# Attended values of a cross-attention kernel: transposed token-major by DMA, and an output projection on scaled 16-bit parts

## The reference

```
q    = x @ W_q                      k_t, v_t  = text @ W_k, text @ W_v
p_t  = softmax(q k_t^T / sqrt(32))  text_out  = p_t v_t
qsem = l2norm(p_t @ text)           sem       = qsem . l2norm(image)
p_ip = softmax(q k_ip^T / sqrt(32) + 0.5 * sem) * mask      ip_out = p_ip v_ip
out  = (text_out + ip_out) @ W_out + b_out + x
```

## Time and profile before

| | us |
|---|---|
| median of 3 runs | 1199.03 |
| profiled execution, whole | 1194.57 |
| its span | 1192.8 |
| busy DVE | 959.0 (80%) |
| busy ACT | 726.2 (61%) |
| busy POOL | 533.0 (45%) |
| busy DMA engines, queue q1 | 54.9% |

### The profile page before, as it was taken

How to read it: one execution, slowest core, us unless ns; L and a number is a source line. 1 busy time by engine, 2 the same in 40 slices (tenths; PEclk the granted TensorE clock), 3 DMA queues, 4 the chain that set the end, 5 groups by cost and what they waited for, 6 DMA issues and landing times.

```text
span 1192.8 us, 27846 instructions
## 1 busy us (share of the span) xinstructions
PE 1102.1 (92%) x8149; PEld 977.1 (82%) x8149; DVE 959.0 (80%) x3834; ACT 726.2 (61%) x2299; POOL 533.0 (45%) x1774
## 2 busy tenths in 40 slices
PE   6993777999999999999999999999999999999977
PEld 5862666888888888888988889888888898888867
DVE  3243488889888988989888988988898988898972
ACT  1142576767666666767676767666666767676630
POOL 0001254455554454555455455455445545545540
PEclk9797889999999999999999999999999999999989
DMA  9586645545465657464645546464756474555421
GB/s 298 193 150 151 140 90 117 121 105 150 106 160 125 152 106 157 105 147 107 142 123 126 156 103 161 109 144 97 159 128 164 103 149 120 131 116 106 112 76 56
DMA packets 386607, 156.91 MB, mean 132 GB/s; under 512 B 354057, under 2 KB 363557, under 8 KB 386457
## 3 DMA queue, kind: packets, MB, share of 16 engines
q1 hardware_dynamic: 386457, 155.14, 54.9%
HBM read 43.15 MB, written 28.05 MB: 60 GB/s over the span
## 4 chain that ended last, share of the span: by engine, by line
PE 30%; DVE 24%; issue 9%; DMA 9%; ACT 8%; POOL 8%; SPq 0%; DVEq 0%; ACTq 0%
PE ps_O L1098 12%; PE ps_Q L1065 9%; DMA pts<-ph 9%; ACT pr L812 4%; PE ps_S L1025 4%; DVE smax L911 3%; PE ps_U L1041 3%; ACT ph L775 3%; DVE pr L961 3%; POOL ph L840 3%; DVE xT_lo L889 2%; DVE aT L929 2%; DVE attn L984 2%; DVE n L973 2%; DVE bias L921 2%
## 5 line engine op out<-in xcount | busy, mean ns | idle before, releaser
L812 ACT ACTIVATE pr<-ps_S,bias 128x73 f32<-128x73 f32 x1280 | 305.4, 322 | 260.8 <-DVE bias L921 260.0
L840 POOL TENSOR_TENSOR ph<-pr,ph 128x220 f16<-128x220 f32 (+1 forms) x640 | 281.2, 460 | 312.3 <-ACT ph L775 307.7
L1098 PE MATMUL ps_O<-wo_hi,aT 128*128 128x320 f32 x1240 | 332.1, 325 | 36.2 <-DVE x_in L902 21.5
L775 ACT ACTIVATE ph<-pr 128x292 f16<-128x292 f32 x640 | 252.0, 444 | 65.8 <-DMA pts<-ph 56.8
L1098 PEld LDWEIGHTS ps_O<-wo_hi,aT 128*128 128x128 f32 x1240 | 219.5, 190 | 51.5 <-DVE x_in L902 29.5
L1025 PE MATMUL ps_S<-kbd,qT 128*128 128x308 f32 x960 | 203.0, 321 | 0.9 <-ACT pr L812 0.7
L1098 PE MATMUL ps_O<-wo_lo,aT 128*128 128x320 f32 x620 | 192.7, 311 | 0.0
L1041 PE MATMUL ps_U<-xm,pts 128*128 128x110 f16 (+1 forms) x2560 | 187.4, 216 | 3.7 <-DVE attn L984 2.2
L911 DVE TENSOR_REDUCE smax<-ps_S 128x4 f32<-128x292 f32 x320 | 145.6, 455 | 50.4 <-PE ps_S L1025 50.0
L1065 PE MATMUL ps_Q<-xT_hi,wq_hi 128*128 128x512 f32 x400 | 162.2, 405 | 12.3 <-DVE qT L889 12.2
L1065 PE MATMUL ps_Q<-xT_lo,wq_hi 128*128 128x512 f32 x400 | 165.9, 415 | 0.0
(11 more groups left out here) (169 smaller groups left out, 1629.6 us busy)
## 6 DMA issues: line engine op xcount, KB each, us to landing
x_in<-in_x_dram SPq DMA_DIRECT2D x16, 1280.0 KB, 6.4
out_dram<-x_in SPq DMA_DIRECT2D x64, 320.0 KB, 2.7
pts<-ph SPq DMA_TRANSPOSE x320, 2.8
w_k<-in_L_xattn_W_k_dram SPq DMA_DIRECT2D x5, 512.0 KB, 9.0
w_ip<-in_L_xattn_W_k_ip_dram SPq DMA_DIRECT2D x1, 2560.0 KB, 11.9
w_v<-in_L_xattn_W_v_dram SPq DMA_DIRECT2D x1, 2560.0 KB, 20.8
w_ip<-in_L_xattn_W_v_ip_dram SPq DMA_DIRECT2D x1, 2560.0 KB, 10.3
xm<-x_d SPq DMA_DIRECT2D x20, 110.0 KB
```

The lines of the kernel that those rows point to most:

```text
L775: last = nc.scalar.activation(hi[:, :, col:col + T], pr[u % P_RING][:], ACT.Copy)
L812: last = nc.scalar.activation(pr[t % P_RING][:, h, :], sc[:, h, 0:T], ACT.Exp, bias=bias[t % 2][:, h:h + 1], scale=SCALE)
L840: nc.gpsimd.tensor_tensor(lo, pr[u % P_RING][:, :, t0:t1], one[:, :, 0, t0:t1], ALU.subtract).then_inc(pl_ready, 1)
L1098: last = nc.tensor.matmul(bank[m][:, 0:HALF], stationary[:, q * P:(q + 1) * P], moving, start=(k, a, b_) == O_MMS[0], stop=(k, a, b_) == O ...
```

## The change

The attended values are no longer transposed on TensorE. `attn` (128 tokens x 4 x 128, float32) is split into 16-bit parts as it lies, token by token: ScalarE writes the high part `at16[:, 0]` at s = 0 of the slot two later, GpSimd the low part `at16[:, 1]` (one instruction of 128x512) at s = 1 behind its two pieces of `ph`, and SP issues one DMA transpose of 128x1024 at s = 2 into a ring of 10. The output projection multiplies 16-bit `aT` with 16-bit `wo`, both scaled by powers of two; the image values `vw` and the bias are scaled alike, in float32. Each output add multiplies by `inv_out`. In ScalarE's order the new instruction stands behind L775 and ahead of what `finished` lists and of L812; SP's new transpose stands behind that of `ph` in the same step. In the prologue the high part of `W_out` is made later, and its maximum is taken to find the scale.

```diff
-        if s == 1 and w.has(slot - 2):
-            todo.append(("attn", slot - 2, 0, 0, "M"))
...
+                    if s == 2 and w.has(slot - 2):
+                        m = slot - 2
+                        ring = w.count(SLOTS, m) % AT_RING
+                        sp.wait_ge(at_hi, w.count(SLOTS, m + 1))
+                        sp.wait_ge(at_lo, w.count(SLOTS, m + 1))
+                        if w.has(m - AT_RING):
+                            sp.wait_ge(o_ready, w.count(NI * OUTS, OUTS * ((m - AT_RING) // CC + 1)))
+                        sp.dma_start_transpose(aT[ring][:], at16[m % 2][:].rearrange("p k s c -> p (k s c)")
+                                               ).then_inc(aT_loaded[ring], 16)
...
+                    if s == 0 and w.has(slot - 2):
+                        m = slot - 2
+                        act.wait_ge(attn_ready, w.count(UNITS, SUB * (m + 1)))
+                        if w.has(m - 2):
+                            old = w.count(SLOTS, m - 2)
+                            act.wait_ge(aT_loaded[old % AT_RING], 16 * (old // AT_RING + 1))
+                        nc.scalar.activation(at16[m % 2][:, 0], attn[m % 2][:].rearrange("p s h d -> p s (h d)"),
+                                             ACT.Copy).then_inc(at_hi, 1)
...
-                            nc.scalar.activation(aT[w.count(SLOTS, i) % AT_RING][0][:], ps_M[:], ACT.Copy, scale=inv_sv).then_inc(aT_hi, 1)
...
+                    if s == 1 and w.has(slot - 2):
+                        m = slot - 2
+                        pool.wait_ge(at_hi, w.count(SLOTS, m + 1))
+                        nc.gpsimd.tensor_tensor(at16[m % 2][:, 1], attn[m % 2][:].rearrange("p s h d -> p s (h d)"),
+                                                at16[m % 2][:, 0], ALU.subtract).then_inc(at_lo, 1)
...
-                            nc.vector.tensor_tensor(half, bank[m][:, 0:HALF], half, ALU.add).then_inc(o_added, 1)
+                            nc.vector.scalar_tensor_tensor(out=half, in0=bank[m][:, 0:HALF], scalar=inv_out, in1=half,
+                                                           op0=ALU.mult, op1=ALU.add).then_inc(o_added, 1)
...
-                            nc.vector.scalar_tensor_tensor(out=aT[w.count(SLOTS, i) % AT_RING][1][:], in0=ps_M[:], scalar=inv_sv,
-                                                           in1=aT[w.count(SLOTS, i) % AT_RING][0][:].bitcast(F32),
-                                                           op0=ALU.mult, op1=ALU.subtract).then_inc(aT_lo, 1)
...
-                            for q in range(SUB):
-                                last = nc.tensor.transpose(ps_M[:, q * P:(q + 1) * P],
-                                                           attn[i % 2][:, q].rearrange("p h d -> p (h d)"), ident[:])
...
-                            if part == 0:
-                                pe.wait_ge(aT_lo, w.count(SLOTS, CC * (i + 1)))
+                            for k in ((0, 1, 2), (3, 4))[part] if c == 0 else ():
+                                n = w.count(SLOTS, CC * i + k)
+                                pe.wait_ge(aT_loaded[n % AT_RING], 16 * (n // AT_RING + 1))
```

More of the change, by code:

```diff
@@ L226, in _ @@
                 nc.gpsimd.memset(vip_bd[:], 0.0).then_inc(bd_zero, 1)
-                for k in range(2):
+                for k, (total, own) in enumerate(((2, 0), (14, 13), (3, 1))):
                     pool.wait_ge(local_max, k + 1)
-                    nc.gpsimd.partition_all_reduce(amax[:, 2 + k:3 + k], amax[:, k:k + 1], P, RMAX).then_inc(all_max, 1)
+                    nc.gpsimd.partition_all_reduce(amax[:, total:total + 1], amax[:, own:own + 1], P, RMAX).then_inc(all_max, 1)
             @block.scalar
@@ L554, in main_loop @@
     OUTS = 2 * SUB
-    AT_RING, P_RING, SIP_RING, PH_RING, PT_RING = 9, 5, 3, 2, 3
+    AT_RING, P_RING, SIP_RING, PH_RING, PT_RING = 10, 5, 3, 2, 3
     X_RING = NI
@@ L591, in main_loop @@
     attn = [sb(f"attn{i}", [P, SUB, HG, DH], F32) for i in range(2)]
-    aT = [[sb(f"aT{r}_{k}", [P, TILE], F32R) for k in range(2)] for r in range(AT_RING)]
+    at16 = [sb(f"at16_{i}", [P, 2, SUB, P], F16) for i in range(2)]
+    aT = [sb(f"aT{r}", [P, 2 * SUB, P], F16) for r in range(AT_RING)]
     pip = sb("pip", [P, SUB, IPR + 1], F32)
@@ L611, in main_loop @@
         sem(n) for n in "u_ready nd_done prod_done rd_done n2_done attn_ready".split())
-    aT_ready, aT_hi, aT_lo = sem("aT_ready"), sem("aT_hi_done"), sem("aT_lo_done")
+    at_hi, at_lo = sem("at_hi_done"), sem("at_lo_done")
+    aT_loaded = [sem(f"aT_loaded{r}") for r in range(AT_RING)]
     n2h_done, y0_ready, newton_step, y_ready = (sem(n) for n in "n2h_done y0_ready newton_step y_ready".split())
@@ L672, in emptied @@
         return {"x": (xT_lo, w.count(SLOTS, CC * i + c + 1)), "q": (q_lo, w.count(SLOTS, i + 1)),
-                "attn": (aT_lo, w.count(SLOTS, i + 1)), "ip": (pT_lo, w.count(NI, i + 1)),
+                "ip": (pT_lo, w.count(NI, i + 1)),
                 "out": (o_added, w.count(NI * OUTS, OUTS * i + c + 1))}[kind]
@@ L982, in turn @@
                         if w.has(un - 2) and us == 0:
-                            v.wait_ge(aT_ready, w.count(SLOTS, un - 1))
+                            v.wait_ge(at_hi, w.count(SLOTS, un - 1))
+                            v.wait_ge(at_lo, w.count(SLOTS, un - 1))
                         nc.vector.tensor_tensor(attn[un % 2][:, us], uo[:, :, COL_V:XW],
@@ L1067, in turn @@
                             last.then_inc(q_ready, 1)
-                        elif kind == "attn":
-                            pe.wait_ge(attn_ready, w.count(UNITS, SUB * (i + 1)))
-                            for q in range(SUB):
-                                last = nc.tensor.transpose(ps_M[:, q * P:(q + 1) * P],
-                                                           attn[i % 2][:, q].rearrange("p h d -> p (h d)"), ident[:])
-                            last.then_inc(aT_ready, 1)
                         elif kind == "ip":
```

68 lines of the change are left out of this document (38 added, 30 removed).

## The result

The changed kernel takes 1239.72 us in the median of 4 runs (1236.14 to 1243.81), the kernel before 1199.99 beside it: ratio 1.032, 95% interval 1.028 to 1.036. The change makes the kernel some 40 us slower. The forecast was 1214, 15 us slower: the right side, and 1.3 us inside the range's upper end of 1241, but well short in size. The profiled execution spans 1242.0 us.

What follows compares the result with a forecast made beforehand. A once-per-slot loop of VectorE, ScalarE and GpSimd, 12.36 us without TensorE, was taken as the bound. Terms summed to +0.22 us a slot, +15 us in all: 1209.6 profiled, median 1214 us, 8-in-10 range 1178 to 1241.

Steps and rivals of the forecast that it cites:

- hold by the low part: At s = 1, GpSimd's 128x512 instruction keeps VectorE's f (L968) waiting for its end: +0.70 us a slot, bounds 0.57 to 0.85.
- bias: VectorE's bias of s = 3, held by GpSimd's later first piece of ph: +0.08 us a slot, +0.37 if for both pieces.
- L929 removed: VectorE's L929 leaves what was read as a gapless stretch of the loop: -0.66 us per slot.
- the add: VectorE's output add gets a scalar operand: +0.06 us each, about one in the stretch, so +0.05 us a slot.
- ScalarE's new copy: ScalarE's 128x512 instruction at s = 0 behind L775, 0.6 us long: +0.05 us a slot, bounds 0 to 0.25.
- DMA transposes, with the waits for them: SP's extra transpose per slot, behind the pts transpose, lands two steps ahead of the piece needing it: nothing.
- Rival (a): No hold on VectorE's f (L968), so the loop loses 0.61 us a slot: 1150 us; chance 0.15.
- the gapless stretch: VectorE works without a gap from w_sem to the bias of s = 3, which ends 6.14 us after y.
- The loop without TensorE: Once per slot, from y through VectorE, ScalarE and GpSimd's Newton rounds: 12.36 us, with no instruction of TensorE in it.
- Rival (c): DMA: 80 more transposes make ScalarE wait 0.4 us more a slot for pts transposes: 1246 us; chance 0.15.
- TensorE's relief: Four transposes, 0.43 us per slot, leave TensorE outside the loop; earlier scores give about 2 us less over the run.
- the added waits: ScalarE's for attn_ready at s = 0, GpSimd's for at_hi and SP's for at_lo: nothing.

Runs made afterwards that it cites:

- the stub kernel: The changed kernel with GpSimd's new low-part instruction writing 16 of 512 columns only: 0.999 to the kernel before, 1197.65 us.
- a third kernel: The changed kernel with 16-column low part, all added per-slot pieces left out from the tenth slot on: 0.986; with TensorE's four transposes put back, unread: 0.984.

## Why the prediction was right in its sign and wrong in its size

Steps from kernel to kernel, in us a slot (1% of 1199 us over 80 slots is 0.15), against the terms of the sum:

| term | forecast | measured | from |
|---|---|---|---|
| hold by the low part | +0.70, bias +0.08 | +0.50 (alone in before: +0.70) | 1.032 less 0.999 |
| L929 removed | -0.66 | -0.14 for 0.46 of it on average | 0.991 |
| the same, and three of TensorE's four transposes | -0.66 and 2 us in all | -0.12 | 0.992 |
| the rest of L929 and of the transposes, 16-bit outputs, ScalarE's old copy gone, the prologue | +0.05, for the add | -0.10 | 0.986 less 0.992, intervals overlap |
| ScalarE's new copy (and the stub) | +0.05 | 0.0 | 0.985 less 0.986 |
| DMA transposes, with the waits for them | 0 | +0.21 | 0.999 less 0.985 |

All rows but the second (it is part of the third) add up, as they must, to the whole: +0.48 a slot before rounding, 39 us. The 0.46 is 37 us over 80 slots.

- **The hold** was right in mechanism and place, and with the bias too high in size: 0.78 against 0.50. That the kernel before with the added instruction gave 0.70, just as forecast, is in part luck: that instruction takes 1280 ns and not 1119, f was held 0.95, and ScalarE waited for it too. GpSimd's instruction takes 1158 ns; 1119 came from the slope of the earlier trace rows. f's median is 794 ns against "0.7 us or more", and in the slot shown f ends 0.08 us behind it. The Trainium skill, GPSIMD Engine Reference, Specifications, tells of contention on the shared SBUF interfaces; by that rule, the trace agrees, and adds that the VectorE instruction is not slowed but kept to the other's end. Rival (a) fell with it.
- **L929 is the mis-sized term,** and the largest error. All removals together, with the 16-bit outputs, measured -0.21 (0.986) where I had -0.61: 0.40 us a slot too favourable, and of L929 by itself three tenths came out. With the transposes' 0.21 this outweighs what I had too high elsewhere (hold and bias 0.28, ScalarE's copy 0.05 or so), and leaves the 0.26 by which +0.22 fell short of +0.48. The step that failed was "it lies in the gapless stretch: -0.66 us per slot". The stretch was gapless in the slot that I showed. The slots come in rounds of five with different TensorE work and transfers, and the waits ahead of smax, qT and pipT in the others were not among what I read: of the waits has only ScalarE's for pts and w_sem's for y. Over the run, VectorE could give up 0.52 us a slot and have seven tenths of it waited away at the next wait.
- **The loop without TensorE** was the premise behind that step, and it too was read in one slot. The page of before, part 4, gives the shares of the chain that ended last, over the whole run:

```profile
PE 30%; DVE 24%; issue 9%; DMA 9%; ACT 8%; POOL 8%; SPq 0%; DVEq 0%; ACTq 0%
```

TensorE has more of it than VectorE, and L929 has 2% there, 24 us and not 53. That page would have warned against counting the saving in every slot.

- **The DMA transpose** was put at nothing because it is issued right behind one pts transpose and a step ahead of the next. It costs 17 us in the stub kernel. Rival (c) gave it 32 us through ScalarE's wait for pts, and that wait fell, from 56.8 to 53.0 us. What it costs through is open: TensorE's clock likely has a part, and that the DMA engines can delay a pts transpose is seen only at the load of x.
- **TensorE's relief** was taken as -2 us; alone, and three quarters of it, it measures +5, and in the changed kernel giving the work back gains 10. That less work on an engine that is not in the loop could cost anything was not among the rivals.
- **ScalarE's copy and the added waits** were rightly small. The prologue and the end were not tested by themselves; in the two traces w_sem starts 1.6 us later for the first time (forecast 0), and from its last start to the end there are 2.3 us less (forecast -1).
- **Two sums of the working do not come out.** Twice the slope beyond 220 columns gives 593 + 292 x 3.6 = 1.64 us as the upper bound of the new instruction, not 1.4; nothing else was built on it. The ends of the forecast's range leave out part of the 3 us that its middle takes off: by its own terms they are 1194 and 1239, not 1195 and 1241. The measured 1239.72 lies inside the recorded range and just outside the corrected one, so that it was inside is luck.
- Of the signs named ahead: f, GpSimd's instruction and VectorE's even busy time came as said; TensorE fell to 86%, not 88%; the slot grew by 0.63 in place of 0.2, which pointed at the terms above.

## What to carry to other kernels

A cost that is found on one turn of a loop holds for that turn: before a saving is counted in every turn, look at each kind of turn for the wait that comes next. Here a delay of VectorE counted for some four fifths (40 us of the 48 by which the hold lengthened its busy time) and a saving for three tenths (11 of 37 us). Elementwise work given to GpSimd is not free beside VectorE: half or more of its length can land on one small VectorE instruction with two SBUF inputs (0.60 of 1.16 us, 0.95 of 1.28). A DMA transpose whose own result is early can still cost time, here 17 us for 70 of them in one kernel; measure it by leaving it out, and with the clock of TensorE in view, before it is put at nothing.

## What the runs showed of the hardware that I had not expected

- Taking work from TensorE can slow a kernel: 44 us of low clock in the changed kernel and none before, and 10 us gained by putting unread transposes back (1.032 to 1.024, and 0.999 to 0.990), but none in a third kernel that had 24 us of it.
- After a 2.28 us wait of TensorE the granted clock was 0.52 in the next stretch, in which the scores took 1.12 us instead of 0.66.
- A GpSimd subtraction takes 428 ns for 128 columns and 1158 for 512, so four pieces cost 0.55 us more than one. An estimate from the two: 1.9 ns a column and 185 ns that do not depend on the columns.
